# First attention of a two-layer transformer kernel: another order of its tiles on TensorE, and the row of maxima scaled on VectorE

## The reference, cut to what matters

```
x   = layer_norm(context input);  lat = layer_norm(normalised latents)
q = lat @ Wq;  k, v = split(concat([x, lat]) @ Wkv)
dots = einsum(q, k) * 64 ** -0.5
attn = softmax(dots)                    # over all keys: 512 tokens and 32 context rows
out  = einsum(attn, v) @ Wout
```

## Time and profile before

| | us |
|---|---|
| median of 3 runs | 777.03 (776.41 to 777.33) |
| profiled execution | 778.1, of which the span is 776.2 |
| PE busy in the span | 694.8 (90%) |
| DVE / ACT / POOL busy | 472.0 (61%) / 394.4 (51%) / 378.5 (49%) |
| the rounds of the first attention | about 28.7 to 505 |

### The profile page before, as it was taken

How to read it: one execution, slowest core, us unless ns; L and a number is a source line. 1 busy time by engine, 2 the same in 40 slices (tenths; PEclk the granted TensorE clock), 3 DMA queues, 4 the chain that set the end, 5 groups by cost and what they waited for, 6 DMA issues and landing times. The chain is left out here.

```text
span 776.2 us, 13776 instructions
## 1 busy us (share of the span) xinstructions
PE 694.8 (90%) x4714; PEld 421.3 (54%) x4714; DVE 472.0 (61%) x966; ACT 394.4 (51%) x676; POOL 378.5 (49%) x362
## 2 busy tenths in 40 slices
PE   4899999999999999999999999997899378559991
PEld 3654555545556546545545545557799134336661
DVE  4735474775776676578468558475343459856553
ACT  4575664564655555555465464434464255234440
POOL 7164373464454565543475455444333403766552
PEclk9999999999999999999999999999999599659997
DMA  9999999999000000000030003310210700123325
GB/s 247 182 185 185 177 188 107 3 4 4 1 1 1 2 15 1 1 1 2 2 122 2 1 1 81 124 45 12 73 43 25 223 2 11 46 69 90 85 64 179
DMA packets 109866, 50.60 MB, mean 65 GB/s; under 512 B 44804, under 2 KB 103048, under 8 KB 109800
## 3 DMA queue, kind: packets, MB, share of 16 engines
q1 hardware_dynamic: 106280, 42.46, 40.7%
q0 software_dynamic: 3520, 7.27, 2.8%
HBM read 20.07 MB, written 29.64 MB: 64 GB/s over the span
## 5 line engine op out<-in xcount | busy, mean ns | idle before, releaser
L873 ACT ACTIVATE PT<-PSUM 128x1024 f32<-128x1024 f32 x128 | 128.7, 1025 | 131.4 <-PE PSUM L1636 131.1
L692 POOL TENSOR_TENSOR PSUMS<-PT 128x1024 f32<-128x1024 f32 x32 | 76.1, 2377 | 204.8 <-ACT PT L873 166.2
L692 POOL TENSOR_TENSOR PSUMS<-PSUMS,PT 128x1024 f32<-128x1024 f32 x62 | 150.5, 2427 | 16.7 <-ACT PT L873 9.8
L1261 DVE TENSOR_REDUCE TOPS<-PSUM 128x2 f32<-128x1024 f32 x128 | 151.5, 1219 | 7.6 <-PE PSUM L1605 7.0
L1668 PE MATMUL PSUM<-PT,BIG 128*64 128x512 f32 x512 | 130.6, 611 | 0.0
L1216 DVE TENSOR_TENSOR SIL<-SIL,PSUM 128x256 f32<-128x256 f32 (+1 forms) x62 | 32.2, 519 | 61.7 <-ACT SIL L785 61.7
L1251 DVE TENSOR_TENSOR KL<-PSUM,KH 128x512 fp32r<-128x512 f32 x32 | 22.1, 690 | 68.8 <-ACT KH L846 68.6
L1605 PE MATMUL PSUM<-KH,QH 64*128 64x512 f32 x256 | 58.5, 454 | 2.6 <-DVE QL L1254 2.6
L785 ACT ACTIVATE SIL<-PSUM 128x256 f32<-128x256 f32 (+1 forms) x62 | 28.7, 463 | 57.7 <-PE PSUM L1470 34.7
L1668 PEld LDWEIGHTS PSUM<-PT,BIG 128*64 128x64 f32 x512 | 28.4, 135 | 53.0 <-issue 51.6
L1605 PEld LDWEIGHTS PSUM<-KH,QH 64*128 64x128 f32 x256 | 24.4, 185 | 58.3 <-DVE TOPS L1261 24.7
(11 more groups left out here) (257 smaller groups left out, 1347.2 us busy)
## 6 DMA issues: line engine op xcount, KB each, us to landing
lists_d<-EMPTY SPq DMA_DIRECT2D x3, 2730.0 KB, 39.5
lists_b<-EMPTY SPq DMA_DIRECT2D x3, 2470.0 KB, 35.0
lists_d<-EMPTY SPq DMA_DIRECT2D x1, 2665.0 KB, 37.0
XG<-lists_d SPq DMA_DIRECT2D x39, 65.0 KB, 1.9
lists_b<-EMPTY SPq DMA_DIRECT2D x1, 2405.0 KB, 18.0
BIG<-in_L_ffn_w SPq DMA_DIRECT2D x1, 2048.0 KB, 8.5
W2ALL<-in_L_ffn_w SPq DMA_DIRECT2D x4, 512.0 KB, 6.3
PT<-results_d SPq DMA_DIRECT2D x8, 256.0 KB, 4.8
```

The source lines that it names most:

```text
L692: pool.tensor_tensor(PSUMS[:, i % 2], PTT[:, i % 2, 0] if kt == 1 else PSUMS[:, i % 2], PTT[:, i % 2, kt], ALU.add).then_inc(s_ps, 1)
L873: act.activation(PTT[:, i % 2, kt], PSUM[:, place:place + 2, :], ACT.Exp, scale=DH ** -0.5).then_inc(s_exp, 1)
L1261: dve.tensor_reduce(TOPS[:, c, 0, :], PSUM[:, place:place + 2, :], AX.X, ALU.max).then_inc(s_max, 1)
```

## The change

The list `ITERATION` gets a new order. p2 moves from behind t1 up to p0 and p1, so that three `pv` tiles stand together. s1 moves from behind t2 to before it. p3 moves from behind t3 to before it. t4 moves from before s2 to behind it. In the rounds that have them, P0 and P2 stand around s3 and no longer ahead of s2.

The step `max_turn` is cut in two. The joining reduction on DVE becomes a step `row_max` (rm), directly behind t4. TOPROW is then made by DVE in one instruction, from the transposed maxima broadcast over the four tiles and OWN_TILE broadcast over the columns, and ACT's four instructions are gone. In the list, DVE's new instruction stands at mt.

```diff
--- before.py
+++ after.py
@@ -319,7 +319,7 @@
 
 
         ITERATION = (
-            "E A B PC CA0 C CA1 O0 ADD CS V qk p0 p1 t0 s0 t1 p2 t2 D s1 t3 p3 t4 P0 P2 s2 s3 rows mt O1 OUT "
+            "E A B PC CA0 C CA1 O0 ADD CS V qk p0 p1 p2 t0 s0 t1 s1 t2 D p3 t3 s2 t4 rm P0 s3 P2 rows mt O1 OUT "
             "O2 O3").split()
 
         beside = [{} for _ in range(ALL + 1)]
@@ -369,15 +369,15 @@
 
         first_top = [("top", (0, c)) for c in range(TOPS_OF)]
         order = [("qk", 0), ("context_keys", 1)] + first_top[0:2] + [("values", (0, 0))] + first_top[2:4] + [("values", (0, 1))]
-        order += first_top[4:] + [("max_turn", 0), ("context_kept", 1), ("counters", 0)]
+        order += first_top[4:] + [("row_max", 0), ("max_turn", 0), ("context_kept", 1), ("counters", 0)]
 
         instead = [[("values", (0, 2))], [], [("values", (0, 3))], [("context_values", 0), ("spread_rounded", 0)]]
         for i in range(ALL):
             for at in ITERATION:
                 if at[0] == "s":
                     order.append(("scores", (i, int(at[1]))))
-                elif at in ("qk", "mt") and i + 1 < ALL:
-                    order.append(("qk" if at == "qk" else "max_turn", i + 1))
+                elif at in ("qk", "rm", "mt") and i + 1 < ALL:
+                    order.append(({"qk": "qk", "rm": "row_max", "mt": "max_turn"}[at], i + 1))
                 elif at[0] == "t" and i + 1 < ALL:
                     order.append(("top", (i + 1, int(at[1]))))
                 elif at[0] == "p":
@@ -847,16 +847,6 @@
                     if a >= GROUP:
                         act.wait_ge(s_sc, context_of(a // GROUP - 1))
                     act.activation(QF[:, a % GROUP, :], PSUM[:, place, :], ACT.Copy).then_inc(s_qkh, 1)
-                elif name == "max_turn":
-                    act.wait_ge(s_topt, a + 1)
-                    if a >= GROUP:
-                        act.wait_ge(s_sc, context_of(a // GROUP - 1))
-                    if a == 0:
-                        act.wait_ge(*CONST.at(0, "own"))
-                    for t in range(TPB):
-                        last = act.activation(TOPROW[:, a % GROUP, t * P:(t + 1) * P], PSUM[:, place, 0:P], ACT.Copy,
-                                              scale=OWN_TILE[:, t:t + 1])
-                    last.then_inc(s_toprow, 1)
                 elif name == "scores":
                     i, kt = a
                     act.wait_ge(s_sc, SCORED[name, a])
@@ -1263,7 +1253,7 @@
                         dve.tensor_reduce(TOPS[:, :, 1, :].rearrange("p t h -> p h t"),
                                           PSUM[:, place:place + 2, 0:TPB * M].rearrange("p h (t n) -> p h t n", t=TPB),
                                           AX.X, ALU.max).then_inc(s_max, 1)
-                elif name == "max_turn":
+                elif name == "row_max":
                     dve.wait_ge(s_max, TOPS_OF * (a + 1))
                     if a:
                         dve.wait_ge(s_topt, a)
@@ -1271,6 +1261,15 @@
                         dve.wait_ge(*CONST.at(0, "topt"))
                     dve.tensor_reduce(TOPT[:, :].rearrange("p (h n) -> p n h", h=2)[:, 0:TPB, :],
                                       TOPS[:, :, :, :].rearrange("p t a h -> p t h a"), AX.X, ALU.max).then_inc(s_comb, 1)
+                elif name == "max_turn":
+                    dve.wait_ge(s_topt, a + 1)
+                    if a == 0:
+                        dve.wait_ge(*CONST.at(0, "own"))
+                    if a >= GROUP:
+                        dve.wait_ge(s_sc, context_of(a // GROUP - 1))
+                    dve.tensor_tensor(TOPROW[:, a % GROUP, :].rearrange("p (t n) -> p t n", t=TPB),
+                                      PSUM[:, place, 0:P].unsqueeze(1).broadcast_to([P, TPB, P]),
+                                      OWN_TILE[:, :].unsqueeze(2).broadcast_to([P, TPB, P]), ALU.mult).then_inc(s_toprow, 1)
                 elif name == "one_over":
                     g, c = a
                     cols = slice(c * P, (c + 1) * P)
```

## The result

| | before | after |
|---|---|---|
| median (4 runs each) | 777.18 (776.41 to 779.78) | 816.05 (810.08 to 818.59) |
| ratio, 95% interval | | 1.0483 [1.0421, 1.0545] |
| profiled execution, its span | 778.1, 776.2 | 816.26, 814.5 |
| second attention's first keys and values on PE start at | 513.84 | 547.89 |

The change costs 38.9 us where 14 were forecast. The direction is right, the size is not, and the range of 781 to 800 misses it. The last line of the table places it: 34.05 us are lost up to that point, and 4.2 us between it and the end of the span (262.4 before, 266.6 after). Measured from the first transpose of maxima to the last, which leaves out the start of the kernel, the loss is 36.1 us (462.3 before, 498.4 after).

The account below looks back on a forecast made before the run. PE, busy 460 of 466 us, was taken to bound the first attention. From the profiled 778.1, the terms (largest +11.4 plain rounds, +6.7 reciprocals) summed to 792.3, forecast as 791.3 because that execution lay 1.1 above the median; range 781 to 800.

Parts of the forecast that it names:

- Part 1: p2 joins p0 and p1 on PE: three tiles take 2.71, saving about 0.36 a round, 11 us over 31 rounds.
- Parts 2 and 3: PE waits for banks at s1 (0.38) and s3 (0.28), each plus 0.08; plain round +0.38, +11.4 over 30 rounds.
- Part 4: TOPROW on DVE: waits behind context_sums go (-0.8), but later reciprocals delay RECS, QH and KH in O rounds (+6.7).
- Part 5: Rounds with own waits: 9, 17, 25, 29 -1.8; a_split +1.3; steps at D -1.2; round 0 -0.8; round 31 -0.6.
- Rival (d): The new DVE instruction is caught behind POOL, by the shared read port: 799 us, chance 0.1.
- (a): Rival: faster, banks come free in time at s1 and PE keeps 0.46 a round; 764 us, chance 0.07.
- (b): Rival: only one wait bites, t4 and the dearer first pair fill the one at s3; 780.5 us, chance 0.08.
- (c): Rival: the reciprocals hide because ACT and DVE have slack, so the 6.7 cost is nothing; 784.6 us, chance 0.2.
- (e): Rival: the order does nothing, gain and wait cancel in each round; 777 us, chance 0.05.

Follow-up runs that it names:

- short additions: Changed kernel with POOL's additions cut from 1024 to 32 columns a partition from the third pair on (timing only, output wrong): 790.97 us, ratio 1.0164.
- the control: Kernel before the change with the same cut of POOL's additions to 32 columns (timing only, output wrong): 776.51 us, ratio 0.9961.

## Why the prediction was right in direction and wrong in size

**Part 1, right.** Three weighted sums take 2.73 (2.71 was forecast; forecasts stand in brackets below too).

**Parts 2 and 3, right, with one term too dear.** t0 to s1 and t3 to s3 are 1.91 each (1.90), and the waits are released by DVE TOPS as said; first weighted sum to transpose is 10.05 (9.95). But the next queries start 0.09 behind the transpose, where before it was 0.35. They take t4's banks now and no longer those of s2, and the experiments show this as the reason. In the kernel before, the weight load of these queries (144.18) is released by ACT PT, the exponential of s2. The distance stays 0.35 with TOPROW alone on DVE, and is 0.08 with the order alone and 0.09 with only t4 moved. That gives part of it back: rounds 1, 2 and 8 are 0.24 longer, not 0.38. Over 30 rounds this term was some 4 us too high. s1's idle time shows as 0.24 and not 0.38, because the row of t1 counts 0.40 as busy where I counted 0.23; s1's start is as forecast. Round 0, which I had at 0.8 less, is 0.9 shorter.

**Part 4, right in mechanism, too small by the hold.** RECS goes ahead of QH, KH releases t0 and QL the next, as written. The waits view of the changed kernel shows both, and the new waits of scores for maxima:

```profile
PE PSUM L1635 <- DVE TOPS L1251: 19.0, 35, 2.4
ACT RECS L888 <- DVE REC L1280: 17.1, 7, 2.4
...
PE PSUM L1604 <- ACT KH L846: 2.9, 4, 0.8
PE PSUM L1611 <- DVE PLACE L1078: 2.8, 2, 1.4
PE PSUM L1604 <- DVE QL L1244: 2.1, 2, 1.8
```

Rounds 10 and 18 lost 1.7 and 1.6 where the sum had 1.5 (1.1, and 0.38 as in every round). In round 26 RECS itself was caught, as its timeline shows:

```profile
445.28 4.87 POOL L692 TENSOR_TENSOR PSUMS<-PSUMS,PT 128x1024 f32<-128x1024 f32 x2
...
447.88 2.81 DVE L1286 TENSOR_TENSOR RECS<-REC,RECS 64x512 fp32r<-64x512 f32 x1 [0.69 <-ACT RECS L888]
...
452.16 0.80 PE L1604 MATMUL PSUM<-KH,QH 64*128 64x512 f32 x2 [1.78 <-DVE QL L1244]
...
453.85 0.66 PE L1635 MATMUL PSUM<-QH,KL 64*128 64x512 f32 x2
454.28 0.66 PE L1635 MATMUL PSUM<-QL,KH 64*128 64x512 f32 x2
```

2.81 instead of 0.69, a wait of 1.78 at t1, then matmuls 0.43 apart: 5.9 us in one round.

**Part 5, the step that failed.** Rounds 9, 17 and 25 came out as forecast (13.47 against 13.48). The a_split rounds did not: "one more DVE instruction (0.6) ... +0.45 each, +1.3". I took XTL's 0.6 from its old place and carried it to a new one without asking what runs on POOL there. It takes 2.45, PE waits 2.39, and the clock falls: 10.4 us in rounds 3, 11 and 19 and 5.2 in the rounds behind them, of which 3.7 and 0.8 stay with short additions. The router rounds at D were in the sum with a gain of 0.24 each (one passage on PE less); they lost 6.3 in rounds 15 and 23 and 1.1 behind them, of which 1.5 and 0.5 stay. The source view of ROUT after:

```profile
L1057 DVE TENSOR_TENSOR ROUT<-ROUT,RSM x4: 182/2072/2149, 276.9 to 568.8; 128x32 f32<-128x32 f32 x4
```

where the same instruction was 182 ns at its median before. Its own work is 0.18; the rest is the addition beside it. The short additions show that holds, here and in part 4, are nearly the whole of the error: the rounds are 21.4 shorter with them, and the sum of the prediction is met within 1.4 us (1.7 against the control). That it is met so closely is in part luck, since errors cancel. The plain rounds are better than summed, and so are the rounds with O1 to O3 (8.3 against the control, where the sum had 6.7 and seven times 0.38, 9.4). The seven rounds with `context_scores` (3, 7, 11 to 27) are worse, 6.8 where the sum had 3.5. Even 7 and 27, where no router or a_split instruction stands at D, lose 0.8 and not 0.24; the prediction had no term for this, and no run isolates it.

**Rival (d), right mechanism, wrong victim.** I weighed the shared port for the one instruction that the diff adds, and wrote "the new DVE instruction is caught behind POOL: 799". TOPROW reads one operand from PSUM and was never held, though 27 of its 32 start while additions run. Its group in the changed kernel's groups by line:

```profile
L1270 DVE TENSOR_TENSOR TOPROW<-PSUM,OWN_TILE 128x512 fp32r<-128x512 f32 x32 | 22.1, 692 | 40.7 <-PE PSUM L1617 40.5
```

692 ns is the mean of all 32. The instructions that were caught are not in the diff; the diff moved them against POOL's time, by moving s1 ahead of D (XTL, ROUT) and by putting TOPROW ahead of the reciprocals (RECS). The earlier trace rows had the sign of it: 0.19 at the median and 1.82 at the most, of an instruction of the very kind of ROUT. A sharper rule than the one I used stands in the Trainium skill ("SBUF — State Buffer", Who interferes with whom): a DVE instruction with two inputs in the core's memory contends with a GpSimd instruction that reads it, and one with at most one such input does not, outside the modes in which DVE uses both of its ports. The trace agrees for two inputs (XTL, ROUT and RECS up to 2.45, 2.15 and 2.81 us beside an addition of 2.4) and for three instructions with at most one (TOPROW 0.69, QL 0.68, the reciprocals unchanged). By that rule and the row of POOL's addition, an estimate of XTL would have been up to 0.68 + 2.38 instead of 0.6, before any run.

Two rows of the kernel before show that the count of inputs is not enough to go by. This cast has one input and takes 0.17 clear of the additions; whether it runs in such a mode no run here shows.

```profile
266.92 4.92 POOL L692 TENSOR_TENSOR PSUMS<-PSUMS,PT 128x1024 f32<-128x1024 f32 x2 [0.42 <-ACT PT L873]
266.96 2.38 DVE L1099 CAST SLOT<-RSM 128x4 int32<-128x4 f32 x1
```

And it is not always DVE that pays. In the kernel before, RECS of round 26 starts at 418.90, between two additions, and takes 0.69. Those two additions, from 416.48, take 5.35 together. In the six rounds where RECS falls so, the pair takes 5.33 to 5.35, and the other pairs in the stage take 4.88 to 4.93. So RECS stood close to the additions before the change too, and part 4 moved it from a gap between them into one.

**Rivals (a), (b), (c), (e)** are excluded: both waits are there, the reciprocals do not hide, and the kernel is slower by far more than its noise.

**Left open.** The 4.2 us lost after the attention: the granted clock from 550 on is 0.85 where it was 0.87 in the like stretch before, but no run isolates it. Rounds 16 and 24 stay long by 1.6 and 1.1 with D ahead of s1, and the trace of that run shows holds there too: PLACE takes 2.31 in one, PLACE 1.00 and SLOT 2.23 in the other, and PE waits 0.71 and 0.29 for QL behind them. Why 12 and 20 stay 0.5 long was not followed up. The kernel before takes 779 in one group of runs and 789 in the others. The profiled kernels put that difference behind the attention: from the last transpose to the end of the span they take 284 to 287 us in the first group, 294 to 298 in the second and 299 to 300 in the third, whatever the order. Its cause is open. Ratios from different groups are therefore less sharp than their intervals say.

## What to carry to other kernels

When an order is changed, list not only what each engine's new neighbours are, but which DVE instructions that read and write only the core's memory, those with two operands first, now fall inside a running POOL instruction; each can cost the rest of that instruction, and what stands behind it on DVE pays. Price a moved instruction at its new place: its duration in the old trace holds only beside the old neighbours. A bank pair that is released by DVE needs its full hold (here 1.90 us from matmul to matmul) covered by PE's work between two takers, and an instruction that waits for PE should stand neither ahead of DVE work that others need nor behind work that is slow or can be held.

## What the runs showed of the hardware that I had not expected

- A short DVE instruction pays for the whole rest of POOL's: ROUT (128x32) went from 0.18 to 2.15, XTL (128x512) from 0.68 to 2.45, RECS from 0.69 to 2.81, each ending 0.1 to 0.5 after the addition did. The additions that they waited for kept their 2.37 to 2.44; the next one behind XTL, which started at 209.78 while XTL was still running, took 2.54.
- One wait of 2.39 us on PE in an otherwise full stretch was followed, 1.9 us after PE had started again, by some 3 us at 1.2 GHz (matmuls 0.43 apart, 213.3 to 216.3). So the rounds with a hold of 1.8 on DVE lost 3.1 to 3.7 us and the next ones 1.2 to 2.1, where 1.0 to 1.4 and 0.3 stay with short additions.
